# Feed-forward tiles of the first layer: the product of the rounded magnitudes with their block scales on POOL in place of VectorE

## The reference, cut to what matters

```python
def fake_quant_nvfp4(x, global_scale):
    xb = x.reshape(sh[:-1] + (sh[-1] // BLOCK, BLOCK))
    amax = jnp.max(jnp.abs(xb), axis=-1, keepdims=True)
    sc = jnp.clip(amax / FP4_MAX * global_scale, 0.0, FP8_MAX)
    sc8 = sc.astype(jnp.float8_e4m3fn).astype(jnp.float32)
    dq = sc8 / global_scale
    safe_dq = jnp.where(dq == 0.0, 1.0, dq)
    a = jnp.clip(jnp.abs(xb) / safe_dq, 0.0, FP4_MAX)
    q = jnp.sign(xb) * _FP4_VALS[jnp.digitize(a, _FP4_MIDS)]
    return (q * dq).reshape(sh)

hidden = jax.nn.silu(gate_out) * up_out       # (1088, 1024)
return nvfp4_linear(hidden, down_w, s_in_down[0])
```

## Time and profile before

| | |
|---|---|
| median of three runs | 654.71 us (654.02 to 655.57) |
| profiled execution | 650.81 us |
| its span in the trace | 648.7 us |
| TensorE, VectorE, ScalarE, POOL busy | 522.9, 428.2, 361.2, 222.7 us |
| mean granted TensorE clock | 0.905 of full speed |

### The profile page before, as it was taken

The page is one execution under the profiler, slowest core; times in us unless marked ns, Lnnn a source line. Parts: engine busy times, 40 slices in busy tenths (PEclk is TensorE's granted clock), DMA queues, the critical chain, the costliest instruction groups (busy, mean ns, idle before and its releaser), DMA issues.

```text
span 648.7 us, 9820 instructions
## 1 busy us (share of the span) xinstructions
PE 522.9 (81%) x3178; PEld 427.2 (66%) x3182; DVE 428.2 (66%) x982; ACT 361.2 (56%) x894; POOL 222.7 (34%) x234
## 2 busy tenths in 40 slices
PE   3944956066635979999999999999999999999936
PEld 2733844023323879999999987787777777787625
DVE  5949997999998264445564442285767777775626
ACT  1637654345445746776766733743667666677610
POOL 2021001022422610122201124126677777777710
PEclk9985888577875789999999999999999999999969
DMA  8970000007300000000000000210678777877557
GB/s 277 383 268 1 1 0 0 0 2 253 84 2 0 1 25 25 26 25 3 24 26 1 1 0 2 70 26 1 186 214 237 212 228 213 250 237 226 140 234 257
DMA packets 44054, 67.44 MB, mean 104 GB/s; under 512 B 11149, under 2 KB 27142, under 8 KB 43876
## 3 DMA queue, kind: packets, MB, share of 16 engines
q1 hardware_dynamic: 36836, 64.62, 31.3%
q0 software_dynamic: 7168, 2.20, 1.8%
HBM read 66.81 MB, written 17.72 MB: 130 GB/s over the span
## 4 chain that ended last, share of the span: by engine, by line
PE 51%; DVE 28%; DMA 6%; ACT 5%; issue 5%; POOL 4%; SPq 1%; POOLq 0%; DVEq 0%
PE ps L1073 10%; PE ps L726 5%; PE ps L727 5%; PE ps L728 5%; PE ps L937 5%; PE ps L895 5%; DVE region L1725 3%; PE ps L1063 2%; DMA region<-y_rows 2%; PE ps L926 2%; PE ps L909 2%; PE ps L802 2%; DVE region L1669 2%; PE ps L1081 2%; DMA region<-ffn_w 1%
## 5 line engine op out<-in xcount | busy, mean ns | idle before, releaser
L1725 DVE TENSOR_TENSOR region<-ps,region 32x136 f32<-32x136 f32 x128 | 38.1, 297 | 73.8 <-PE ps L895 72.3
L1073 PE MATMUL ps<-region 128*128 128x352 f32 x256 | 86.4, 460 | 0.3 <-issue 0.3
L726 PE MATMUL ps<-nTh,high 128*128 128x272 f32 (+2 forms) x248 | 75.3, 304 | 8.7 <-ACT region L1301 8.7
L677 POOL DMA_INDIRECT region<-x_rows,region x64 | 67.3, 1051 | 20.3 <-issue 16.6
L686 POOL DMA_INDIRECT y_rows<-region x64 | 65.4, 1023 | 23.4 <-issue 15.0
L727 PE MATMUL ps<-nTl,high 128*128 128x272 f32 (+2 forms) x248 | 72.5, 293 | 0.0
L636 POOL COPY region<-region 32x544 f32<-32x544 f32 x32 | 26.1, 815 | 133.9 <-DVE region L1744 132.4
L728 PE MATMUL ps<-nTh,pairs_low 128*128 128x272 f32 x192 | 56.2, 293 | 0.0
L726 PEld LDWEIGHTS ps<-nTh,high 128*128 128x128 f32 (+2 forms) x248 | 47.0, 190 | 11.0 <-ACT region L1301 10.2
L1874 DVE SCALAR_TENSOR_TENSOR region<-region,ps 128x176 f32<-128x176 f32 x64 | 25.4, 396 | 43.3 <-ACT region L1390 42.4
L1400 ACT ACTIVATE high<-region 88x512 fp32r<-88x512 f32 x64 | 40.3, 630 | 23.8 <-PE ps L728 23.8
(11 more groups left out here) (250 smaller groups left out, 1371.2 us busy)
## 6 DMA issues: line engine op xcount, KB each, us to landing
region<-moe_w SPq DMA_DIRECT2D x64, 352.0 KB
region<-moe_w SPq DMA_DIRECT2D x64, 176.0 KB
y_rows<-zrow SPq DMA_DIRECT2D x1, 6528.0 KB, 25.4
region<-y_rows SPq DMA_DIRECT2D x8, 768.0 KB, 9.4
region<-wqkv SPq DMA_DIRECT2D x8, 384.0 KB, 3.0
region<-ffn_w SPq DMA_DIRECT2D x2, 1024.0 KB, 8.1
region<-patches SPq DMA_DIRECT2D x3, 384.0 KB, 8.3
region<-patches SPq DMA_DIRECT2D x1, 1152.0 KB, 10.7
```

The source lines that it names most:

```text
L677: nc.gpsimd.indirect_dma_start(out=xb[m8], out_offset=None, in_=x_rows, in_offset=bass.IndirectOffsetOnAxis(ap=sloti[:, at:at + 1], axis=0 ...
L726: nc.tensor.matmul(out, parts_a[0], parts_b[0], start=first, stop=False)
L1073: mm = nc.tensor.matmul(ps[:, 2 + m % 2, 0:2 * EI], xbT[m % 2][:, c, :], w13[m][:, c, :], start=(c == 0), stop=(c == DC - 1))
L1725: last = V.tensor_tensor(sc[r, s0:s0 + 8, 0:T].rearrange("p (a b) t -> p a b t", a=4), ps[r, 4:8, 0:4 * GW].rearrange("p a (b h t) -> p a ...
```

## The change

POOL gets a function `block_multiply(t)`: it waits for a new semaphore `s_hcl`, which VectorE's clamp L1686 now raises, and multiplies `hq[t % 4]` in place with the scales in `hsb[t % 3]`. It raises `s_hq` as L1694 did. POOL calls it for tile t - 2 ahead of the divide of tile t, for tile 7 after the last divide (ahead of `ln(2, 0)`), and for tile 8 behind `ln(2, 0)`. On VectorE L1694 is gone; ahead of L1689, which overwrites a scale buffer that POOL reads, it waits until the product of the tile three back is done. The semaphore `s_omu` is folded into `s_mixz`.

```diff
@@ POOL
+            def block_multiply(t):
+
+                pool.wait_ge(s_hcl, t + 1)
+                q = hq[t % 4].rearrange("p (k c) -> p k c", k=PAIRS)
+                nc.gpsimd.tensor_tensor(q, q, bc(hsb[t % 3], 1, PAIRS), ALU.mult).then_inc(s_hq, 1)
+
             for t in range(NT):
                 if t == 5:
                     pool.wait_ge(s_xqT, 3)
                     nc.gpsimd.memset(qT[:, :, T:SLOT], 0.0).then_inc(s_zero, 1)
                     nc.gpsimd.memset(kbd, 0.0).then_inc(s_zero, 1)
+                if t >= 2:
+                    block_multiply(t - 2)
                 pool.wait_ge(s_hinv, t + 1)
                 v = hid[t % 3].rearrange("p (k b r) -> p k b r", k=PAIRS, r=2)
                 nc.gpsimd.tensor_tensor(v, v, bc(bc(hss[t % 2][:, 2, :], 1, PAIRS), 3, 2), ALU.mult).then_inc(s_hdiv, 1)
                 if t == NT - 1:
+                    block_multiply(t - 1)
                     ln(2, 0)
+            block_multiply(NT - 1)
             ln(2, 1)
@@ ScalarE
-            act.wait_ge(s_omu, 1)
-            act.wait_ge(s_mixz, 3)
+            act.wait_ge(s_mixz, 1)
+            act.wait_ge(s_mixz, 4)
@@ VectorE
-            V.engine_nop().then_inc(s_omu, 1)
+            V.engine_nop().then_inc(s_mixz, 1)
...
-            dve.wait_ge(s_mixz, 3)
+            dve.wait_ge(s_mixz, 4)
...
                 if rounding:
                     after(done_r)
-                    done_r = mark(V.tensor_scalar(q, q, 6.0, -6.0, ALU.min, ALU.max))
+                    V.tensor_scalar(q, q, 6.0, -6.0, ALU.min, ALU.max).then_inc(s_hcl, 1)
                 if scales:
                     after(done_s)
+                    need(dve, s_hq, n - 2)
                     done_s = mark(V.scalar_tensor_tensor(out=neg..., in0=bc(low, 2, 2),
                                                          scalar=E_MAGIC, in1=bc(a1, 2, 2), ...))
-                if rounding:
-                    after(done_r)
-                    q = q.rearrange("p (k c) -> p k c", k=PAIRS)
-                    V.tensor_tensor(q, q, bc(hsb[w % 3], 1, PAIRS), ALU.mult).then_inc(s_hq, 1)
```

More of the change, by code:

```diff
@@ L334, in build @@
         s_d0 = sem("s_d0")
-        s_omu = sem("s_omu")
         s_sq = sem("s_sq")
@@ L366, in build @@
         s_hid = sem("s_hid")
+        s_hcl = sem("s_hcl")
         s_hq = sem("s_hq")
```

## The result

The changed kernel takes **666.66 us** (median of six runs, 664.21 to 668.23) where the kernel before took 654.37 us on the same chip (six runs, 652.0 to 655.57): a ratio of **1.0181, with a 95% interval of 1.0149 to 1.0212**. Slower by 12.3 us, where the prediction said 11.1 us slower (665.8). Both profiled executions lie under their medians: 650.81 us before, 665.43 after, with spans of 648.7 and 663.6.

The account below looks back on a forecast made before the run. VectorE was taken to bound the first layer's feed-forward. Steady tiles +8.7 and tail +2.4 made +11.1 us, added to the 654.71 us median for 665.8 us; own range 664.5 to 667.7, wider range 658.8 to 670.0, chance 0.62.

Parts of the forecast that it names:

- the stage goes at VectorE's pace: First layer's feed-forward: VectorE busy 44.15 of 44.60 us in steady tiles, so its loss or gain per tile is the kernel's.
- Seven savings of 0.60 us: VectorE without L1694 in the seven tiles with both loop halves: 0.60 us each, -4.2 us if nothing else happened.
- POOL's product at 2.13 us: Each of nine moved 128x1024 bf16 products on POOL: taken as long as the divide L615, between 1.03 and 2.29 us.
- (d): Rival, chance 0.05: POOL's bf16 product is cheap, 1.03 us; some +1.2 us in all, 655.9 us.
- (e): Rival, chance 0.05: POOL's bf16 product is dear, 2.9 us; +18 us in all, 672.7 us.
- POOL is first at the port, L1697 is held: Steady tiles: POOL's product holds the small tensor_scalar L1697, loss 1.89 less 0.60 saved; taken +1.24 a tile, +8.7 us.
- The tail, +2.44 us: Last two tiles: ninth tile's L1669 held, +0.95 us; last product then ends on POOL at 207.51 instead of 205.07.
- the list of signs: Expected in the timeline after: L1697 some 2.1 us, tile period 8.5 to 8.6, POOL's product 2.1 to 2.3, ninth L1669 2.2.
- Slack of gate and up products: Steady tiles: later transposes delay ScalarE's next gate, which has 3.5 us of slack; costs nothing, up to 2 us.
- (a): Rival, chance 0.14: L1697 gets the port first, the next tile's L1669 is held; +0.44 a tile, +6.0 in all, 660.7 us.
- (b): Rival, chance 0.08: neither L1697 nor L1699 needs the port; L1669 +0.1 a tile, +3.6 us in all, 658.3 us.
- (c): Rival, chance 0.06: POOL holds VectorE nowhere but in the tail; -4.2 and +0.9, -3.3 us in all, 651.4 us.

Follow-up runs that it names:

- three variants: Changed kernel with the product released by L1704, with L1704 writing an accumulator, or with half the product left on VectorE: 1.0148, 1.0057, 1.0074 of the kernel before.
- the accumulator form: Changed kernel with the small tensor_scalar L1704 also writing an accumulator to a column no longer read, nothing else changed: 1.0057 of the kernel before, stage 80.17 us.

## Why the prediction was right, point by point

- **That the stage goes at VectorE's pace**: right. The 11.4 us by which the stage grew are the bulk of the 12.3 us of the median.
- **Seven savings of 0.60 us**: mis-sized. With L1694 gone L1704 starts 0.65 us after the clamp's start (183.23 to 183.88), L1697 had started 1.14 after it (163.04 to 164.18): the saving is 0.49. Most of the missing 0.11 us stands between L1700 and L1704 (0.31 us from start to start, where L1694 had followed L1689 after 0.21): L1704 needs L1700's result, and L1694 had hidden that. The prediction used both figures, 0.60 for the saving and 163.69 for the start, which is 0.49 before the old 164.18, without noticing that they don't agree.
- **POOL's product at 2.13 us**: right, 2.12 us in all nine (2114 to 2120 ns). bf16 is neither cheaper nor dearer here than f32; rivals (d) and (e) are out.
- **POOL is first at the port, L1697 is held**: right in all seven tiles. The hold itself was taken 0.1 us too long, since L1700 did not delay POOL at all (0.08 us from the clamp's end to POOL's start, as before). 1.77 us of hold less 0.49 of saving is +1.28 us a tile, where the prediction had 1.89 less 0.60, or 1.19 without the 0.1, and took 1.24. Two errors of 0.1 us cancelled, which is luck in the size and not in the mechanism. Up to the clamp of the eighth tile the stage lost 8.95 us, 7 x 1.28; predicted 8.7.
- **The tail, +2.44 us**: right, 2.41. L1679 of the ninth tile took 2.89 us, not the 2.2 written in the list of signs, because it was asked for earlier; its end is what counts, and that is 0.95 us later against the clamp as worked out.
- **Slack of gate and up products**: right for this change (0.7 us of waits before and after), since a tile of 8.6 us leaves VectorE late enough. In the three variants that shortened the tile and kept TensorE's order the slack was gone, at 1.7 to 3 us.
- **Rivals (a) and (b)**: not what happened, but each could be made to happen, by releasing the product from L1704 and by the accumulator form. The hold that (a) gives L1679 (1.0 us) came out as written, that of (b) at 0.5 in the steady tiles and not 0.7. The stages came out longer, since both left out TensorE's order.
- **Rival (c), no hold**: out, by seven rows of 2.01 us.
- **Not foreseen**: the luck of L1456 and the memsets, 3.0 us in the profiled execution. The spans of the two profiled executions differ by 14.9 us: 11.4 in the stage, 2.35 from there to the first gather, 2.0 behind the last scatter (a stretch of 28.6 to 32.5 us that varies between executions whatever the kernel), less 0.8 elsewhere. The medians differ by 12.3. Between the predicted +11.1 and the measured +12.3 lies 1.2 us, of which the tiles explain 0.25; the rest is within the interval (9.7 to 13.9 us), and how much of it is the memsets' luck stays open.

## What to carry to other kernels

In this kernel, work moved from VectorE to POOL was off VectorE's path only as long as VectorE had work to do meanwhile that POOL does not hold (here the product from PSUM, the addition, the maxima and the reciprocal). Add up that cover for a loop step first: here 2.6 us behind the reciprocal, nearly filled by the 2.1 us that POOL did already, so a second 2.1 us had no place. Look for the loss in the duration of the smallest instructions, not in idle time, and when you shorten one engine's loop, check which in-order queue the moved result now stands in front of.

## What the runs showed of the hardware that was not expected

- A 64-column tensor_scalar is held by POOL's product in its plain form (2.01 us) and not in the form with an accumulator (0.28 us and 0.08 for reading it). A reciprocal of 64 columns is not held (0.55 us).
- A waiting VectorE operation does not always get in between two POOL instructions. L1456, a tensor_scalar from SBUF to SBUF, waited to the end of the fourth memset in one execution (4.58 us) and was let in after the second in another (0.87). L1679, which reads two tensors of SBUF, waited for the end of the product of the seventh tile and then held POOL's next instruction: in four kernels the divide L623 behind it took 3.10 us instead of 2.12, as here in the kernel with the accumulator form, POOL first and then VectorE:

```profile
196.12 2.12 POOL L612 TENSOR_TENSOR region<-region 128x1024 bf16<-128x1024 bf16 x1 [3.16 <-DVE region L1696]
198.19 3.10 POOL L623 TENSOR_TENSOR region<-region 128x1024 f32<-128x1024 f32 x1
```

```profile
197.38 1.94 DVE L1679 SCALAR_TENSOR_TENSOR region<-region 128x1024 f32<-128x1024 bf16 x1
```
